# Graph network on one core: carries over a counted run of columns, source rows scattered in slots of four columns, and all relation rows ahead of the attention carry

## The reference, cut to what matters

```python
x = _layernorm(x + _L0(x, src, dst))                 # 10 steps: gather f[src], segment_sum over dst
x = _layernorm(x + _L1(x, edge_index, w, fc_w, ...)) # attention: softmax over the edges of one src, sums of w-projected x[dst]
x = _layernorm(x + _L2(x, weight, ..., src, dst, edge_type_86))  # relation messages, segment_sum over dst, self loop
x = _layernorm(x + _L3(x, edge_weight, edge_index))  # sum over dst of x[src] * edge_weight
# _L2:  msg = einsum('eb,ebo->eo', w_comp[etype], einsum('ei,bio->ebo', h[src], weight))
#       a = tanh(relu(sum((h[src] @ A1.T + A1_b) * (h[dst] @ A2.T + A2_b + rel_emb[etype])) / sqrt(32)))
#       nei = segment_sum(a * msg, dst)
```

## Time and profile before

| | |
|---|---|
| median of 3 runs | 2836.77 us (2835.66 to 2837.78) |
| profiled execution | 2836.26 us, span 2834.5 us |
| busy in the span | DVE 2001.7 us (71%), POOL 1726.3 (61%), ACT 621.8 (22%), PE 536.7 (19%) |
| DMA | 101.69 MB, 36 GB/s over the span |
| PE clock granted over the span | 0.573 of full speed |

### The profile page before, as it was taken

How to read it: one execution, slowest core, us unless ns; L and a number is a source line. 1 busy time by engine, 2 the same in 40 slices (tenths; PEclk the granted TensorE clock), 3 DMA queues, 4 the chain that set the end, 5 groups by cost and what they waited for, 6 DMA issues and landing times.

```text
span 2834.5 us, 24933 instructions
## 1 busy us (share of the span) xinstructions
PE 536.7 (19%) x3578; PEld 340.6 (12%) x3578; DVE 2001.7 (71%) x3750; ACT 621.8 (22%) x1382; POOL 1726.3 (61%) x1741
## 2 busy tenths in 40 slices
PE   5760000471000000000003032320355450000000
PEld 3330000371000000000003011210122220000000
DVE  7777888788735555528998574279778788678772
ACT  7972333130000000000003023431333430100000
POOL 6777767777466665544757776650465550707776
PEclk9995555796555555555556565555555555555555
DMA  6003332100121122212121101110000001110000
GB/s 222 13 12 99 99 94 83 31 13 12 57 13 30 19 20 24 28 10 103 24 64 21 60 10 10 59 60 0 5 7 6 7 8 46 23 3 10 9 9 9
DMA packets 100895, 101.69 MB, mean 36 GB/s; under 512 B 58169, under 2 KB 92649, under 8 KB 98929
## 3 DMA queue, kind: packets, MB, share of 16 engines
q0 software_dynamic: 53664, 20.91, 8.1%
q1 hardware_dynamic: 46864, 80.15, 7.9%
q10 hardware_dynamic: 320, 0.20, 0.0%
HBM read 38.06 MB, written 60.81 MB: 35 GB/s over the span
## 4 chain that ended last, share of the span: by engine, by line
DVE 41%; issue 18%; POOL 12%; DMA 8%; PE 6%; ACT 3%; DVEq 3%; ACTq 1%; POOLq 0%; SPq 0%
POOL ring L780 3%; POOL cring L475 3%; POOL out_dram L491 2%; DVE YW L1258 2%; DMA cring<-sums_by_list,cidx 2%; DVE RB L1258 1%; PE banks L2701 1%; POOL attention_by_edge L880 1%; POOL ring L873 1%; DVE banks L1089 1%; DVE banks L1099 1%; DVE SW L1095 1%; DVE SW L1094 1%; DVE SW L1104 1%; DVE SW L1389 1%
## 5 line engine op out<-in xcount | busy, mean ns | idle before, releaser
L491 POOL DMA_INDIRECT out_dram<-ring,ridx x196 | 210.5, 1074 | 128.6 <-DVE ridx L2181 68.5
L500 POOL DMA_INDIRECT XS<-in_x_dram,xsi x196 | 199.7, 1019 | 70.2 <-issue 62.3
L500 POOL DMA_INDIRECT SW<-node_table,srci x196 | 200.3, 1022 | 66.1 <-issue 66.1
L500 POOL DMA_INDIRECT XD<-in_x_dram,xdi x196 | 196.1, 1001 | 62.7 <-issue 62.7
L899 POOL DMA_INDIRECT out_dram<-z4w,oidx x98 | 96.3, 982 | 223.9 <-ACT oidx L2455 194.2
L475 POOL DMA_INDIRECT cring<-sums_by_list,cidx x128 | 123.6, 966 | 106.7 <-issue 76.3
L2570 PE MATMUL banks<-tl,dcar 128*128 128x32 f32 (+1 forms) x14 | 4.4, 404 | 779.4 <-DVEq L1371 596.4
L2488 PE MATMUL banks<-YW 128*128 128x392 f16 x784 | 140.3, 333 | 45.3 <-ACT YW L2265 45.3
L780 POOL DMA_INDIRECT ring<-x_by_edge,aidx x96 | 101.0, 1052 | 58.9 <-issue 28.5
L2240 ACT ACT_TABLE_LOAD x22 | 28.2, 1283 | 411.6 <-DVEq L1059 411.6
L1002 DVE TENSOR_SCALAR YW<-YW,b_d 128x784 f16<-128x784 f16 x196 | 82.7, 422 | 46.8 <-PE banks L2488 44.8
(11 more groups left out here) (602 smaller groups left out, 3438.6 us busy)
## 6 DMA issues: line engine op xcount, KB each, us to landing
SW<-in_x_dram SPq DMA_DIRECT2D x20, 625.0 KB
out_dram<-SW SPq DMA_DIRECT2D x20, 625.0 KB
sums_by_list<-RB SPq DMA_DIRECT2D x2, 1800.0 KB
sums_by_edge<-RB SPq DMA_DIRECT2D x1, 3528.0 KB, 9.8
sums_by_list<-RB SPq DMA_DIRECT2D x2, 1600.0 KB
XS<-in_x_dram,xsi POOLq DMA_INDIRECT x196
list_values_by_edge<-RB SPq DMA_DIRECT2D x1, 3136.0 KB
attention_by_edge<-RB SPq DMA_DIRECT2D x1, 3136.0 KB
```

What stands on the lines that cost most here:

```text
L491: pool.indirect_dma_start(out=table, out_offset=off, in_=ring_row(h, j, w), in_offset=None, bounds_check=limit, oob_is_err=False).then_inc ...
L500: pool.indirect_dma_start(out=dest[:, t * w:(t + 1) * w], out_offset=None, in_=table, in_offset=bass.IndirectOffsetOnAxis(ap=idx[:, t:t + ...
```

## The change

1. **Counted run.** After the link matrices, the kernel counts the longest run of columns that a carry has to reach: the leading run of a partition that continues an earlier one, the trailing run that goes on into a later one, and the highest number of edges that share a source. PE and DVE take the maximum over the partitions (`column_max`), DVE turns it into a number of trips of 28 columns (at least 1) in `trips_i[5]` and loads it.
2. **`carry_run`.** In place of the 32 instructions, the carry is added per trip with two instructions on 28 columns (product of flags and the carry in PSUM into `prods`, then the addition). `last=True` starts from the right end. It replaces the 32 instructions in the three sums over destinations and in both spreads over destinations, the loop of `list_carry` (lists 0 and 1), and the loop after the sorted `segment_sums`, there with one further instruction for the last column. The copy of the flags to `pfirst` is left out where `carry_run` is used, and so is the copy of the carry to `car`.
3. **Slots of four columns.** ACT fills slots of 4 columns in place of 14. The first seven are filled during the layer norm of `XS`; then each relation group fills one, between its copies of the transposes and the copy of the self-loop term. POOL scatters slot by slot; the landing counts are kept in three groups of slots, (0,1), (2,3) and (4,5,6).
4. **Rows.** `ROWS_BEHIND` is gone: PE makes 41 rows in place of 31 between the carries `sbak` and `dbak`, and none behind.
5. Some semaphores are merged (`s_zr`, `s_base`, `s_pay`); waits on them move to counts of others. SP issues the same DMAs in the same order.

```diff
+            st.do(V.tensor_reduce(runs[:, 0:1], dbak[:, :], AX.X, ALU.max))
+            st.do(V.tensor_reduce(runs[:, 1:2], dfirst[:, :], AX.X, ALU.add))
+            st.do(V.tensor_scalar(t1[:, :], dstf[:, :], dstf[:, T - 1:T], None, ALU.is_equal))
+            st.do(V.scalar_tensor_tensor(out=t2[:, :], in0=srcf[:, :], scalar=float(N), in1=NS3[:, :, 3], op0=ALU.is_lt,
+                                         op1=ALU.mult))
+            st.wait()
+            st.do(V.tensor_reduce(runs[:, 2:3], t1[:, :], AX.X, ALU.add))
+            st.do(V.tensor_reduce(runs[:, 3:4], t2[:, :], AX.X, ALU.max))
+            st.do(V.tensor_tensor(runs[:, 1:2], runs[:, 1:2], runs[:, 0:1], ALU.mult))
+            st.wait()
+            st.seq(V.scalar_tensor_tensor(out=runs[:, 2:3], in0=runs[:, 2:3], scalar=tm[:, 0:1], in1=runs[:, 3:4],
+                                          op0=ALU.mult, op1=ALU.max))
+            st.seq(V.tensor_tensor(tl[:, 0:1], runs[:, 1:2], runs[:, 2:3], ALU.max))
+            column_max(car[:, 0:1])
+            st.seq(V.tensor_scalar(runs[:, 0:1], car[:, 0:1], (RC0 - 1) / 2, 1.0 / RC0, ALU.add, ALU.mult))
+            st.seq(V.tensor_scalar(runs[:, 0:1], runs[:, 0:1], MAGIC, None, ALU.add))
+            st.seq(V.tensor_scalar(trips_i[5][:, :], runs[:, 0:1], -MAGIC, 1.0, ALU.add, ALU.max))
+            rn = Steps(dve, s_run, dve.value_load(trips_i[5][0:1, 0:1], min_val=1, max_val=ROUNDS))
+
+            def carry_run(flat, flags, w=D, last=False):
+
+                with rn.trip_loop(2) as i:
+                    at_ = i * -RC0 + (T - RC0) if last else i * RC0
+                    e = prods[:, :, :].rearrange("p a b -> p (a b)")[:, 0:RC0 * D].rearrange("p (t d) -> p t d", d=D)
+                    rows = flat[:, bass.ds(at_ * w, RC0 * w)].rearrange("p (t d) -> p t d", d=w)[:, :, 0:D]
+                    rn.seq(V.tensor_tensor(e, flags[:, bass.ds(at_, RC0)].unsqueeze(2).to_broadcast([P, RC0, D]),
+                                           mid(bank[7][:, 0:D], RC0), ALU.mult))
+                    dve.sem_inc(tick, 1)
+                    rn.seq(V.tensor_tensor(rows, rows, e, ALU.add))
+                    dve.sem_inc(tick, 1)
...
-            segment_sums(Y3, S3, D, dmask, dfirst)
+            sums_of_dst(Y3, S3, S)
...
-            segment_sums(SA3, SA3, D, smask, sfirst, T=CW, enter=add_first)
+            segment_sums(SA3, SA3, D, smask, sfirst, T=CW, enter=enter_sorted)
...
-            def out_src_fill(slot_, b):
-
-                for t in range(U):
-                    A.activation(oring[b][:, t * D:(t + 1) * D], XS[:, bass.ds(slot_ * (U * D) + t * D, D)], ACT.Copy,
-                                 scale=rr[:, bass.ds(slot_ * U + t, 1)])
+            def out_src_fill(g, j):
+
+                for t in range(GT):
+                    A.activation(oring_row(j, t), XS[:, bass.ds(g * (GT * D) + t * D, D)], ACT.Copy,
+                                 scale=rr[:, bass.ds(g * GT + t, 1)])
+                A.activation(oidx[:, j * GT:(j + 1) * GT], osi[:, bass.ds(g * GT, GT)], ACT.Copy).then_inc(s_oslot, 1)
+
+            def first_slots(i):
+
+                for j in {1: (0, 1), 2: (2,), 3: (3,), 4: (4,), 5: (5,), 6: (6,)}.get(i, ()):
+                    out_src_fill(j, j)
...
-            with pe.Fori(0, NG - 2 * ROWS_AHEAD - ROWS_BEHIND) as g:
+            with pe.Fori(0, NG - 2 * ROWS_AHEAD) as g:
                 relation_row(g + 2 * ROWS_AHEAD)
             carry(dbak, D)
-            with pe.Fori(0, ROWS_BEHIND) as g:
-                relation_row(g + (NG - ROWS_BEHIND))
```

More of the change, by code:

```diff
@@ L915, in _ @@
             pool.wait_ge(s_heldw, 16)
-            for b in range(2):
-                pool.wait_ge(s_oland[b], 16 * U * ROUNDS)
+            for m, of_slot in enumerate(SLOT_GROUPS):
+                pool.wait_ge(s_oland[m], 16 * GT * len(of_slot) * ROUNDS)
             for h in range(2):
@@ L1377, in segment_sums @@
                 st.do(V.tensor_copy(pmask[:, 0:T], mask[:, :]))
-                st.do(V.tensor_copy(pfirst[:, 0:T], first[:, :]))
+                if not enter:
+                    st.do(V.tensor_copy(pfirst[:, 0:T], first[:, :]))
                 st.wait()
@@ L1663, in list_carry @@
                 dve.sem_inc(tick, 1)
[L1664 to L1671, removed]
+                carry_run(z, lfirst, zw)
             st.do(V.tensor_scalar(t1[:, :], ginf[:, :], float(ZROW), None, ALU.is_lt))
@@ L1695, in _ @@
+            sums_of_dst = lambda src3, dst3, flat: segment_sums(src3, dst3, D, dmask, dfirst,
+                                                                enter=lambda first: carry_run(flat, first))
+            spread_of_dst = lambda: spread_back(S3, D, dend, dstf, enter=lambda flags: carry_run(S, flags, last=True))
             st.seq(V.tensor_scalar(t2[:, :], NS3[:, :, 1], 0.0, None, ALU.is_equal))
@@ L2023, in add_first, with enter_sorted @@
                     dve.sem_inc(tick, 1)
-            segment_sums(SA3, SA3, D, smask, sfirst, T=CW, enter=add_first)
+            def enter_sorted(first):
+                carry_run(SA, first)
+                st.seq(V.scalar_tensor_tensor(out=SA3[:, CW - 1, :], in0=bank[7][:, 0:D], scalar=first[:, CW - 1:CW],
+                                              in1=SA3[:, CW - 1, :], op0=ALU.mult, op1=ALU.add))
+            segment_sums(SA3, SA3, D, smask, sfirst, T=CW, enter=enter_sorted)
             spread_back(SA3, D, send, ks, T=CW, t1=t1c, t2=t2c, enter=add_first)
@@ L2428, in _ @@
             norm_acts(XD, sq_2)
-            norm_acts(XS, sq_2, both=True)
+            def out_src_fill(g, j):
+                for t in range(GT):
+                    A.activation(oring_row(j, t), XS[:, bass.ds(g * (GT * D) + t * D, D)], ACT.Copy,
[4 more added lines that the diff above has]
+                    out_src_fill(j, j)
+            norm_acts(XS, sq_2, first_slots, both=True)
             act.wait_ge(s_grp, 1)
@@ L2433, in _, with relation_group @@
             stage(1, XD3, 0, 0)
[L2435 removed]
+            def relation_group(g, j, last, slot_next=None):
                 b = j % 2
@@ L2573, in _ @@
             key_rows(3)
-            carry(dcar, D)
             column_row(4)
@@ L2577, in _ @@
             column_row(5)
+            carry(dcar, D)
+            column_row(6)
             carry(dcar, 1)
             carry(dbak, 1)
-            column_row(6)
+            column_row(7)
             carry(dcar, D)
```

85 lines of the change are left out of this document (44 added, 41 removed).

## The result

The changed kernel takes **2752.2 us** (median of 4 runs, 2749.7 to 2754.8) against 2837.1 before in the same comparison: a ratio of 0.9701, 95% interval 0.9685 to 0.9718. Run again later, beside other kernels, it took 2755.4, ratio 0.9717 (0.9703 to 0.9730). Its first profiled execution took 2749.7 us, span 2748.0, and is the one shown here.

The account below looks back on a forecast made before the run. The prediction took a chain of waits split over all engines (DVE, POOL's gathers and DMA handing over) as the bound. Terms +5.2 - 36.6 - 8.3 - 2.1 - 7.2 + 3.4 - 40.0 = -85.6 from 2836.3 gave 2750 us, range 2738 to 2766.

Parts of the forecast that it names:

- The carries: Each carry_run one trip, 2.8 us; three sums over destinations save 12.2 us each, 36.6 in all, list 0 saves 8.3.
- rival 3: Padding in the last partition lengthens the counted run: three more trips in 14 carries give 2876 us; chance 0.02.
- The count: Finding the longest run, with DVE alone on the path: cost +5.2 us (2.2 ahead, 3.0 tail), bounds +3.5 and +7.
- First spread: DVE saves 12.65 us, but SP's write of x1_by_edge is next limit, so path gains 7.2; bounds 7.2 and 12.65.
- rival 2: SP is not the limit of the first spread and centring in the attention spread hides: 2735 us; chance 0.06.
- Relation rows: Attention spread: DVE waits some 30 us for the carry and centring is exposed, net cost 3.4 us; bounds -6.7 and +8.
- Source slots: Relation stage: slot fills hide in ACT's waits, removing DVE's waits at round starts; gain 40.0 us, bounds 34 and 41.
- 5.16 comes back there and about 0.5 at the next product: Relation stage, each of six later round starts: DVE's wait for PE goes, 5.65 us gained per round.
- Rival 1: Relation stage: ACT's slot fills do not hide, the 40 us gain falls away, 2790 us; chance 0.09.
- The rule weighed against a row: Norm of XS beside POOL's scatters: profile rows show DVE losing nothing, the skill's blocking rule says it could; 0 added.
- Rival 4: POOL's scatters block DVE's two-input instructions in the norm of XS: +15 us, 2765; chance 0.05.
- list 1: List carries of two trips, now one carry_run each: 0.3 us saved seven times, 2.1 in all.

Follow-up runs that it names:

- Experiment 5: Changed kernel with at least two trips in every carry_run, one more than needed: 2790.1 us, ratio 0.9842 to the kernel before.
- experiment 8: Changed kernel with SP's write of x1_by_edge put ahead of the last two moves of list rows: 2749.8 us, ratio 0.9699 to the kernel before.
- experiments 2 to 4 and 9: Relation rows reordered: changed kernel with 10 behind carry dbak 2747.2 us, 5 behind 2741.0, more in PE's gaps 2727.2; kernel before with none behind 2860.7.
- experiment 6: Changed kernel with the source slots of 14 columns from the kernel before: 2789.5 us, ratio 0.9837 to the kernel before.

## Why the prediction was right, point by point

**The carries** were right to 0.3 us per sum: 2.8 us for a pair, one trip, and all three sums alone on the path. Experiment 5 prices a trip at 2.98 us and shows which of the 14 carries reach the end: all but the first spread, where rival 3 had counted all 14. Rival 3 is out (one trip).

**The count** was put 0.6 us too dear. The instructions ahead took 2.2 us, as put; the tail (maximum, three small instructions, load of the register) took 2.3 in place of the 3.0 read from the count of list 0. There DVE waits 1.17 us behind its last small instruction, here 0.68.

**First spread.** SP as the limit held: -7.7 for -7.2, shown by SP's unawaited write, by the further trip that disappears there, and by experiment 8. In the twelve profiles with the write in its old place the fetch begins 10.4 to 11.4 us after the write's issue, in the two with the early write 12.1 and 12.4. In the nine whose landings were read it begins 1.3 to 1.6 us behind the landing of the write and 0.8 to 1.1 behind that of the indices; which of the two ends POOL's wait is not told apart. The half of rival 2 that rests on SP falls; the other half, that centring hides, falls with the bare centring at 1840.54.

**Relation rows.** The mechanism held (32.6 us of wait for 30, centring bare), the size was 1.5 us too small. I let the stream start 6.7 us earlier after the fetch; by the marks it was 5.3. The sorted carry and the copy to `pfirst` gave the 6.7, but DVE's shift against the fetch was already 1.1 us smaller ahead of them, and 0.2 more went by `sbak`. The term was small only because two large ones met: a carry shortened by 13 us under a wait, and an order that costs 11 us against a better one. I said the order "costs 3.4 us net" and did not ask what the best order would give; experiments 2 to 4 and 9 do.

**Source slots.** The step that was off is "5.16 comes back there and about 0.5 at the next product". A round's start went from 12.38 to 7.58 us from one `pq` to the next, 4.80, since DVE now waits 0.36 us for its addition; the product gave 0.51. That is 5.3 for 5.65, six times. At the first group DVE's wait fell from 8.8 to 3.5, 5.3 in place of 6.1; the two fills had begun 0.4 us before DVE arrived, and the other 0.4 was not traced. Together, by the shifts, 36.7 for 40.0, inside the bounds; experiment 6 gives 36.4. Rival 1 falls: 42 fills lie in ACT's waits, and a group takes 6.06 us before and after.

**The rule weighed against a row.** During the norm of `XS` POOL scatters from 1914.9 on. Timelines of POOL and DVE there:

```profile
1923.36 1.90 POOL L900 DMA_INDIRECT out_dram<-z4w,oidx  x1 [0.30 <-issue]
```

```profile
1923.30 1.09 DVE L2077 TENSOR_TENSOR XS<-XS,b_bias 128x896 f32<-128x896 f32 x1
1924.43 1.09 DVE L1486 TENSOR_REDUCE banks<-XS 128x28 f32<-128x896 f32 x1
```

DVE's two-input instructions over 896 elements took 1.09 us, all of them, in the 50 us beside these scatters (one cast with a single input took 0.82 in place of 0.63); POOL's instruction took 1.90 us in place of 0.98. Rival 4 is out. A long case in the sorted fetch, timelines of POOL and DVE:

```profile
1453.11 6.34 POOL L781 DMA_INDIRECT ring<-x_by_edge,aidx  x1 [0.30 <-issue]
```

```profile
1451.94 6.69 DVE L1965 SCALAR_TENSOR_TENSOR XS<-XS,YW 128x6272 f32<-128x6272 f32 x1
```

In the profile there are 84 places where an indirect DMA instruction of POOL began 0.06 us or more behind a DVE instruction with two SBUF inputs (over 896 or 6272 elements) and at least 0.05 before its end. In all of them POOL's ended 0.8 to 0.9 us behind the end of DVE's, as if nearly all of its usual 0.94 to 0.98 us came only then. Where DVE's began behind POOL's or within 0.03 us of it, DVE's took 1.15 us at most over 896 elements, in place of 1.09. The Trainium skill (SBUF — State Buffer, "Who interferes with whom") has the second to issue blocked in full; these lines agree for POOL, also in the earlier trace rows, where it began second too. They do not show it for DVE, which lost 0.06 us at most when it began second.

**What was luck.** The span fell by 86.5 us, 0.9 from the sum. Two terms came out dearer than put (slots 3.3, relation rows 1.5), the others cheaper (list 1 0.7, count 0.6, sums and first spread 0.5 each), and 3.3 us more were not in the sum, 1.9 of which belong to a fetch that varies. By the median the changed kernel is 2 us above the 2750 forecast, and run again 5 us: so close a sum is luck, the terms are not. The merged semaphores were not tested by themselves; nothing in the table needs them.

## What to carry to other kernels

When a long piece of work shrinks, the orders that were written around it are due for a new look: here ten rows behind a carry were 22 us better than none with 16 us of carry, and too many with 3, none behind was 11 us worse than five, and the idle gaps ahead of two other carries held four more rows. An engine that waits in the middle of its program (ACT at the self-loop copy) delays everything queued behind that wait; moving the waiting instruction one group later was worth 25 us, though DVE's idle time for it was never more than 0.5 us at once. A gain bought by reordering a DMA queue has to be checked against what then travels beside the moved transfer.

## What the runs showed of the hardware

A loop of one trip cost DVE hardly anything: 0.25 us between dependent instructions, as elsewhere, and 0.55 between two trips. The same 96 gathers took 133.4 to 136.3 us from profile to profile with nothing changed in them, more than several of the terms above; the marks around them, not the totals, told the edits apart. When POOL's indirect DMA instruction began second beside a DVE instruction with two SBUF inputs, it waited that instruction out (up to 6.99 us for 0.94); beside DVE instructions of the same two sizes with one of two inputs in PSUM, none of POOL's took more than 1.01 us in the changed kernel's profile. In SP's queue, 2 KB loads issued 1.2 us behind the 3.1 MB write landed 0.2 us behind it, 8.1 us after their issue, and in experiment 8 a 64 KB move issued 0.7 us behind it took 10.2 us, where such moves ahead of the write took 1.8 to 3.3. PE's granted clock over the span was 0.572 to 0.578 of full speed in all profiled executions. In the stretch of relation rows behind the fetch it was 0.50 (the lower level, 1.2 GHz) in every profile looked at, before and after, and in the relation groups 0.55 to 0.57, so the clock tells none of these kernels from another.
